# Attention values: four heads of a group in four column strips of TensorE, eight heads to a PSUM bank, one normalisation per eight heads

## The reference

```python
x = x + 0.5 * ffn(layernorm(x))     # gated feed-forward, 4-bit weights, 1376 inner channels
x = x + attention(layernorm(x))
x = x + 0.5 * ffn(layernorm(x))     # the same feed-forward again

def attention(h):                   # 32 heads of 16 channels; one key and one value head for all
    qkv = h @ Wqkv                  # 512 + 16 + 16 columns
    scores = q @ k.T / 4 + slope[head] * (pos_k - pos_q),   causal mask
    attn = softmax(scores) @ v      # per head: 256 x 256 times 256 x 16
    return attn.reshape(B, S, 512) @ Wo
```

## Time and profile before

| | us |
|---|---|
| median of three runs (lowest, highest) | 716.85 (716.47, 717.89) |
| profiled execution, span of the engines | 715.8 |
| TensorE (PE) busy | 662.9 |
| VectorE (DVE) busy | 398.6 |
| ScalarE (ACT) busy | 301.8 |
| GpSimd (POOL) busy | 64.0 |
| attention, from group 2 to the last transposes | 282 to 521 |

### The profile page before, as it was taken

How to read it: one execution, slowest core, us unless ns; L and a number is a source line. 1 busy time by engine, 2 the same in 40 slices (tenths; PEclk the granted TensorE clock), 3 DMA queues, 4 the chain that set the end, 5 groups by cost and what they waited for, 6 DMA issues and landing times.

```text
span 715.8 us, 8942 instructions
## 1 busy us (share of the span) xinstructions
PE 662.9 (93%) x3166; PEld 490.6 (69%) x3166; DVE 398.6 (56%) x905; ACT 301.8 (42%) x841; POOL 64.0 (9%) x51
## 2 busy tenths in 40 slices
PE   0259999999999997999999999999999999999998
PEld 0136666677888774775776677567568888788886
DVE  6996677764321248779659768899411114421113
ACT  0543322222111128788878878789411111211111
POOL 5163343320000000000000000000000000000000
PEclk9997999999999999999999999999999999999999
DMA  6112222219500010102002000200089000100001
GB/s 197 38 44 71 76 76 76 74 29 334 227 1 1 0 30 0 30 1 60 1 1 59 2 1 8 53 1 2 1 220 235 1 0 1 60 0 1 1 0 59
DMA packets 39967, 37.09 MB, mean 52 GB/s; under 512 B 9974, under 2 KB 34562, under 8 KB 39284
## 3 DMA queue, kind: packets, MB, share of 16 engines
q1 hardware_dynamic: 39708, 36.20, 17.9%
q10 hardware_dynamic: 216, 0.33, 0.2%
HBM read 22.11 MB, written 10.22 MB: 45 GB/s over the span
## 4 chain that ended last, share of the span: by engine, by line
PE 81%; DVE 13%; ACT 2%; issue 2%; DMA 1%; SPq 0%; DVEq 0%
PE bank L1037 33%; PE bank L1052 15%; PE bank L1136 8%; PE bank L1119 5%; PE bank L1152 4%; PE bank L1083 4%; PE bank L1138 3%; PE bank L1109 2%; DVE sc L850 2%; PE bank L1012 2%; DVE zint L709 2%; DVE sraw L746 1%; PE bank L1145 1%; DVE nmax L859 1%; PE bank L1063 1%
## 5 line engine op out<-in xcount | busy, mean ns | idle before, releaser
L1037 PE MATMUL bank<-xt,w_b 128*128 128x512 f32 (+1 forms) x768 | 186.0, 396 | 0.0
L1037 PEld LDWEIGHTS bank<-xt,w_b 128*128 128x128 f32 (+1 forms) x768 | 140.6, 185 | 34.9
L662 DVE TENSOR_TENSOR hf<-sil,bank 128x512 f32<-128x512 f32 (+1 forms) x44 | 30.2, 687 | 190.2 <-PE bank L1037 190.2
L1052 PE MATMUL bank<-w_d,hs 128*128 128x512 f32 (+1 forms) x528 | 130.7, 397 | 0.9 <-ACT hs L428 0.9
L512 ACT ACTIVATE sc<-sc,nmax 128x128 f32<-128x128 f32 (+1 forms) x256 | 114.0, 449 | 32.2 <-DVE nmax L859 32.0
L1052 PEld LDWEIGHTS bank<-w_d,hs 128*128 128x128 f32 (+1 forms) x528 | 99.1, 188 | 22.7 <-ACT hs L428 1.1
L850 DVE SCALAR_TENSOR_TENSOR sc<-dist,bank 128x128 f32<-128x128 f32 (+1 forms) x256 | 76.0, 349 | 41.6 <-PE bank L1109 23.3
L420 ACT ACTIVATE sil<-bank 128x512 f32<-128x512 f32 (+1 forms) x44 | 26.3, 598 | 135.9 <-PE bank L1037 135.9
L1136 PE MATMUL bank<-pt,vp 128*64 128x256 f32 x256 | 80.9, 398 | 0.0
L428 ACT CAST hs<-hf 128x512 fp32r<-128x512 f32 (+1 forms) x44 | 27.4, 622 | 118.6 <-DVE hf L662 118.6
L1037 PE MATMUL bank<-xt,w_a 128*128 128x512 f32 x288 | 72.6, 409 | 0.0
(11 more groups left out here) (93 smaller groups left out, 623.8 us busy)
## 6 DMA issues: line engine op xcount, KB each, us to landing
gate_up_tail<-w_b SPq DMA_DIRECT2D x1, 7936.0 KB, 25.9
w_b<-gate_up_tail SPq DMA_DIRECT2D x7, 1024.0 KB, 11.0
raw<-in_L_ffn_qweight_gu SPq DMA_DIRECT2D x80, 64.0 KB, 2.3
qp<-qp SPq DMA_DIRECT2D x8, 512.0 KB, 4.2
raw<-in_L_ffn_qweight_down SPq DMA_DIRECT2D x10, 256.0 KB, 3.3
x<-in_L_attn_hidden_states SPq DMA_DIRECT2D x8, 256.0 KB, 3.3
out<-x SPq DMA_DIRECT2D x8, 256.0 KB, 2.2
wqkv<-in_L_attn_Wqkv SPq DMA_DIRECT2D x1, 1024.0 KB, 5.2
```

Of the source, the lines that this page charges most:

```text
L662: nc.vector.tensor_tensor(hf[0:jw(j), n % 2, :], sil[0:jw(j), n % 2, :], up_ps[0:jw(j), :], ALU.mult).then_inc(h_ok, 1)
L1037: ins = nc.tensor.matmul(ps[0:jw(j), :], w_gu(a, k, gu, j), xt[:, b, k, :], start=(k == 0 and q == 0), stop=(k == KT - 1 and q == 2))
L1052: ins = nc.tensor.matmul(acc[t][:, :], hs[0:jw(j), n % 2, a, t * P:(t + 1) * P], w_d[0:jw(j), b, j, :], start=(j == 0 and q == 0), stop=(j ...
```

## The change

The 16 value columns now stand between two stretches of 16 zero columns (`vp` has 48 columns per key tile). A stationary operand is 32 columns of it: zeros behind the values for the even group of a pair, zeros ahead for the odd one. Head i of a group writes partitions 32i to 32i+31, so that the four heads of a group lie in four column strips of the array, and two groups (eight heads, a **pair**) add up in one bank. The first key tile of all four heads runs in step u = 1, the second in u = 2, and nothing in u = 0. The transposes of the inverse sums, `rden_copy` and `normalise` happen once per pair, on 128 partitions. The rows of `wo` are permuted to match, which makes 8 DMAs of one. The value projection makes 16 columns and not four copies of them.

```diff
-    vp = place("vp", [P, 2, 2, 4 * (64 + HD)], F32, 4)
+    vp = place("vp", [P, 2, 2, 3 * HD], F32, 4)
-    inv16 = place("inv16", [P, 2, 8, HD], F32, 4)
+    inv16 = place("inv16", [P, 2, 2, P], F32, 4)
...
-            sp.dma_start(wo[:, :, :], w_o.rearrange("(k p) n -> p k n", p=P)).then_inc(aw_in, 16)
+            wo_rows = w_o.rearrange("(k u i d) n -> u i d k n", u=2, i=4, d=HD)
+            for n in range(8):
+                i, u = divmod(n, 2)
+                sp.dma_start(wo[HD * n:HD * n + HD, :, :], wo_rows[u, i]).then_inc(aw_in, 16)
...
-            def rden_copy(g):
+            def rden_copy(pair):
-                nc.scalar.copy(rden[0:64, g % 2, :], bank[4 + g % 2][0:64, S:2 * S]).then_inc(a_rden, 1)
+                nc.scalar.copy(rden[:, pair % 2, :], bank[4 + pair % 2][:, S:2 * S]).then_inc(a_rden, 1)
...
-                    if u == 0 and m >= 2:
-                        rden_copy(m - 2)
+                    if u == 0 and m >= 3 and m % 2 == 1:
+                        rden_copy((m - 3) // 2)
...
-            def normalise(g):
+            def normalise(pair):
+                b, k = divmod(pair, NPAIR)
+                dve.wait_ge(a_rden, pair + 1)
+                nc.vector.tensor_tensor(at_t[:, b % 2, k, :], bank[4 + pair % 2][:, 0:S],
+                                        rden[:, pair % 2, :], ALU.mult).then_inc(a_norm, 1)
...
-                    v_cols = wqkv[:, k, D + 8 * HD:D + 9 * HD].unsqueeze(1).to_broadcast([P, 4, HD])
+                    ins = nc.tensor.matmul(bank[6][:, S + kt * HD:S + (kt + 1) * HD],
+                                           xa[:, k, kt * P:(kt + 1) * P],
+                                           wqkv[:, k, D + 8 * HD:D + 9 * HD],
...
-            def weighted_values(g, heads):
+            def weighted_values(g, kt):
+                b, pair, u = g // NG, g // 2, g % 2
+                if kt == 0:
                     if g % NG == 0:
                         pe.wait_ge(a_vp, 2 * b + 2)
+                    if u == 0 and pair >= 2:
+                        pe.wait_ge(a_norm, pair - 1)
+                    pe.wait_ge(a_ptc, 3 * g + 3)
+                o = bank[4 + pair % 2]
+                v = vp[:, b % 2, kt, (1 - u) * HD:(3 - u) * HD]
+                for i in range(4):
+                    e = 3 * P * i
+                    if kt == 0:
+                        nc.tensor.matmul(o[32 * i:32 * i + 32, 0:S], v, pt[:, g % 2, e:e + S],
+                                         start=(u == 0), stop=False, skip_group_check=True)
+                    else:
+                        nc.tensor.matmul(o[32 * i:32 * i + 32, P:S], v, pt[:, g % 2, e + S:e + S + P],
+                                         start=False, stop=(u == 1), skip_group_check=True)
+                if kt == 1 and u == 1:
                     pe.wait_ge(a_inv16, g + 1)
                     for t in range(2):
+                        ins = nc.tensor.transpose(o[:, S + t * P:S + (t + 1) * P], inv16[:, pair % 2, t, :],
+                                                  ident[:, :])
...
-                    if m >= 1:
-                        weighted_values(m - 1, (range(0, 2), range(2, 3), range(3, 4))[u])
+                    if m >= 1 and u >= 1:
+                        weighted_values(m - 1, u - 1)
```

More of the change, by code:

```diff
@@ L223, in macaron_block @@
         LAST = NG * B - 1
+        NPAIR = NG // 2
+        LAST_PAIR = NPAIR * B - 1
         first = [lambda t: gu_cols(t, slice(0, P))]
@@ L330, in _ @@
                     sp.dma_start(rows[64:128], rows[0:64]).then_inc(a_qdup[i], 16)
-            sp.wait_ge(a_pv, LAST + 1)
-            sp.wait_ge(a_norm, LAST + 1)
+            sp.wait_ge(a_pv, LAST_PAIR + 1)
+            sp.wait_ge(a_norm, LAST_PAIR + 1)
             for j in range(JA, NJ):
@@ L546, in between @@
                     xt_high(2, g - 3 + u - 1)
-            def rden_copy(g):
-                act.wait_ge(a_pv, g + 1)
-                if g >= 2:
-                    act.wait_ge(a_norm, g - 1)
-                nc.scalar.copy(rden[0:64, g % 2, :], bank[4 + g % 2][0:64, S:2 * S]).then_inc(a_rden, 1)
+            def rden_copy(pair):
+                act.wait_ge(a_pv, pair + 1)
+                if pair >= 2:
+                    act.wait_ge(a_norm, pair - 1)
+                nc.scalar.copy(rden[:, pair % 2, :], bank[4 + pair % 2][:, S:2 * S]).then_inc(a_rden, 1)
             for n in range(3):
@@ L806, in k_low @@
                 for kt in range(2):
-                    v4 = bank[6][:, S + kt * HD * 4:S + (kt + 1) * HD * 4].rearrange("p (h n) -> p h n", h=4)
-                    nc.vector.tensor_copy(strips[:, b % 2, kt, :, 0:HD], v4).then_inc(a_vp, 1)
+                    nc.vector.tensor_copy(vp[:, b % 2, kt, HD:2 * HD],
+                                          bank[6][:, S + kt * HD:S + (kt + 1) * HD]).then_inc(a_vp, 1)
                 for h in range(2):
@@ L867, in inverse_copies @@
             def inverse_copies(g):
+                pair, u = divmod(g, 2)
                 dve.wait_ge(a_inv, g + 1)
-                if g >= 2:
-                    dve.wait_ge(a_pv, g - 1)
-                nc.vector.tensor_copy(inv16[:, g % 2, :, :],
+                if pair >= 2:
+                    dve.wait_ge(a_pv, pair - 1)
+                dst = inv16[:, pair % 2, :, :].rearrange("p t (i n) -> p (t i) n", n=2 * HD)
+                nc.vector.tensor_copy(dst[:, :, u * HD:(u + 1) * HD],
                                       inv[:, g % 2, :].unsqueeze(2).to_broadcast([P, 8, HD]))\
                     .then_inc(a_inv16, 1)
-            def normalise(g):
[L878 to L882, removed]
+            def normalise(pair):
[3 more added lines that the diff above has]
+                                        rden[:, pair % 2, :], ALU.mult).then_inc(a_norm, 1)
             def between(m, u):
@@ L942, in _ @@
                         inverses(m - 1)
-                    if u == 1 and m >= 2:
-                        normalise(m - 2)
+                    if u == 1 and m >= 3 and m % 2 == 1:
+                        normalise((m - 3) // 2)
                     if m < LAST:
@@ L1246, in _ @@
                     exp_transposes(3 * m + u)
-                    if m >= 1:
-                        weighted_values(m - 1, (range(0, 2), range(2, 3), range(3, 4))[u])
+                    if m >= 1 and u >= 1:
+                        weighted_values(m - 1, u - 1)
                     extra(m, u)
-            weighted_values(LAST, range(4))
+            weighted_values(LAST, 0)
+            weighted_values(LAST, 1)
             gate_up(2, 0, 0)
```

31 lines of the change are left out of this document (5 added, 26 removed).

## The result

The changed kernel takes 678.47 us (676.60 to 680.26, 4 runs) against 716.66 (716.18 to 717.89, 4 runs): ratio 0.9458, 95% interval 0.9444 to 0.9473, 38 us less. The span of the profiled execution is 678.2 us (715.8 before); in both cases the profiled execution was the longest of the four (680.26 and 717.89 us).

A forecast was written before the change was run, and what follows sets the result against it. PE was taken as the bound, ScalarE and VectorE 3 to 25% behind. Window gains of 26.6 us, less 2, took the span from 715.8 to 691.2; with 1.05 around it, 692 us, range 684 to 711.

The forecast's parts named there:

- 5 slots for 8 instructions: Value matmuls: second instruction of a head overlaps first of the next; 2.60 us per group becomes 1.62, 0.98 saved.
- all four at once: Rival: instructions queue per strip, PE falls by 2.3 us per group and other engines bind; 682 us, chance 0.05.
- The windows: Five stretches of attention between 282 and 521 us, with forecast gains of 5.2, 8.2, 8.2, 1.2 and 3.8 us.
- the 2 that I took off: Attention: 2 us less gain because values leave step 0 and all stand in steps 1 and 2.
- The 95% limit: Attention windows: VectorE or ScalarE can run at up to 95% busy where it becomes the bound.
- ScalarE's 5.4 us: Group without projections: falls from 5.77 us only to ScalarE's 5.58 - 0.18 = 5.4, a gain of 0.4.
- The case without overlap: Rival: strips take turns, only visits and transposes are saved, 9.5 us; 707 us, chance 0.24.
- the price of a visit: Entering and leaving the 64-column form on PE: 0.24 us, or 0.34 in groups with projections; visits fall from three to two.
- the slower rival: Changing strips costs like entering the form, 0.15 us at six changes per group; 732 us, chance 0.11 including the 774 us extreme.
- The 1.05 us "for what lies around" the span: Added to the forecast span of 691.2 us to give the kernel time of 692 us.
- The rule on weight loads: Loads overlap running matmuls only when row groups differ; here 1.8 us net per group, +57 us, 774 us.
- The edits costed at nothing: Seven more `wo` DMAs shift the spill by 4.3 us, covered by some 60 us; shorter zeroing of `vp` gives nothing.

The follow-up runs named there:

- the run by head: Changed kernel with all values of a group in step 2, head by head, four instructions in a row per strip: 677.64 us.
- the runs with 1.30 and 1.95 us of streaming: Changed kernel with two heads in each of two strips (683.35 us), and with three heads in one strip and the fourth in another (695.28 us).
- the one-strip run: Changed kernel with all four heads of a group in the first column strip, summed there, part of the computation left out: 709.44 us.
- three heads in one: Changed kernel with heads 0, 1 and 2 in the first strip and head 3 in the second, part of the computation left out: 695.28 us.
- the full form without strips: Changed kernel with each head in 128 stationary columns, 16 of values between 112 of zeros, same result: 696.22 us.
- the runs with one visit: Changed kernel with all values of a group in step 2, one visit to the 32-column form: 679.02 us by key tile, 677.64 by head.
- the order by key tile: Changed kernel with all values of a group in step 2, four heads with the first key tile, then four with the second: 679.02 us.
- filler: Changed kernel with the four transposes of every step done twice in groups without projections: 677.39 us.

## Why the prediction was right or wrong

**What failed: "5 slots for 8 instructions".** The bounds had been 0.65 and 2.60 us, and I took 1.62, because I assumed that PE starts instructions strictly in order of the code. The timeline has 0.65 (0.47 and 0.25, less 0.05 of entry in each), and the run by head shows why: an instruction whose strip is free starts although earlier ones wait for a busy strip, with up to three waiting per strip as far as these runs show. On a straight line between the runs with 1.30 and 1.95 us of streaming (683.4 and 695.3), 1.62 would have given 689.2, an estimate. So this term carries 689.2 - 678.5 = 10.7 of the 13.5 us between forecast and result. The rival that had it, all four at once, stood at 682 us with a chance of 0.05. The Trainium skill, "TensorE: Matmul & The Clock Gate", section "Measured speedup vs the span model", gives the span of one matmul plus about 4 ns for each further strip. The trace agrees in kind, with 0.47 us for four strips and 0.43 to 0.48 for one; from strip to strip it has 7 ns, not 4.

**What was off in size: what the other engines allow.** The forecast at 1.62 would have been 3 us too high in any case. The windows give the gains against the forecast's as 6.6 (5.2), 11.5 (8.2), 12.8 (8.2), 1.9 (1.2) and 4.9 (3.8), without the 2 that I took off. The 95% limit was too low for VectorE (98% in the fourth window). The 2 us taken off because the values leave step 0 were tested by no run; the windows gave more than the forecast had even without them. And a group without projections was held at ScalarE's 5.4 us: such a group takes 5.22 us already in the one-strip run (401.82 to 407.04), with ScalarE busy for 4.91 of it, so that part of its work for the group lies outside the group's window on PE. A limit per group is not one where a queue carries work over its edge; only the sum over a batch is.

**Right.** PE set the pace before: with 21 us less of it, from one strip to three heads in one, the time falls by 14 us, and with 21 more off by 12. That is some 60%, so PE's time counts in large part, though not in full over all groups. The case without overlap was put at 707 and measured 709.4. The entry and exit of the narrow form are real: the full form without strips has none and gains 13 us over one strip. The copy of the inverse sums and the product took 373 and 419 ns at 128 partitions, against 367 and 414 at 64: their durations stayed. But the price of a visit was low for groups without projections, 0.33 in place of 0.24, because 0.43 is not what transposes are worth when scores follow them. Changing strips costs nothing like entering the form: the first instructions of the four strips start within 0.02 us, and the slower rival, which needed 0.06 us per change, falls. The 1.05 us "for what lies around" the span were a median of other runs against one run's span: the profiled runs themselves took 2.09 us more than their span before and 2.06 after. For the sum that is worth under 1 us: the median of the changed kernel stands 0.3 us above the profiled span.

**The rule on weight loads** (the Trainium skill, same page, section "The mechanism"). The changed kernel's loads in the visit at 401.12:

```profile
401.11 0.16 PEld L1140 LDWEIGHTS bank<-pt,vp 128*32 128x32 f32 x8 [0.17 <-issue]
```

No load stands open: all eight are done in 0.16 us beside the matmuls, all on the same rows of the array. The rule's 774 us are contradicted by the run as they were by the trace of before. The same section names a second case that the prediction left out: a load into the background weight buffer is pulled ahead too. That would allow what the trace shows; no run here tells whether it is the reason.

**Expected and not so.** PE's clock did not stay at 1.00: 0.86 in the first window, 0.97 in the third and 0.94 in the fourth, where PE now waits for the other engines. The edits costed at nothing (DMAs of `wo`, the memset) left no trace: the windows between 282 us and the end of attention hold all of the change in span.

## What to carry to other kernels

Four float32 matmuls of up to 32 stationary columns each, written to four different groups of 32 partitions, took the time of one, as long as they stood together; count the instructions of the fullest strip. The order in the code did not matter in the two orders tried, with up to four instructions for one strip in a row. Behind six in a row the next strip started 0.46 us late, so take the strips in turn. Collect such matmuls in few places, since every entry and exit of the narrow form is 0.32 to 0.34 us of PE; whether that reaches the time is another matter, as the runs with one visit show. When the bound is a ring of engines, price a cut of one by steps (here 14, 12 and 5 us for three equal cuts of 21), and check the limit of the others over a batch and not over a group.

## What the runs showed of the hardware

- The order of starts: with strips 0, 0, 0, 0, 1, 1, 1, 1, ... in the code, 16 instructions took 0.80 us, exit included, and 0.78 in the order by key tile (401.48 to 402.26 in that run's timeline). With 0, 0, 0, 0, 0, 0, 1, 1 strip 1 started 0.46 us behind strip 0, when the third instruction of strip 0 started.
- A full-form stationary operand of 128 columns is no slower to use than 64 or 32 in this loop: eight instructions take 1.72 us from start to start (407.79 to 409.51), against 1.75 in one strip of 32. It has no entry and exit: 696.2 against 709.4 us with the same streaming.
- Four 128x128 transposes take 0.35 us when scores follow, 0.43 when a plain float32 matmul of the projections follows (403.77 to 404.20 in the run by head), and 0.53 when the narrow form follows.
- The granted clock of PE fell to 1.2 GHz for short stretches in attention once PE had waits there (0.94 over 282 to 460 us, 0.99 with filler), with no change of the time that these runs could tell.
